# Shares of the edges in free PSUM columns, and the mean for rows without an edge by TensorE instead of GpSimd, in a two-layer sparse graph attention kernel

## What is computed

```python
# layer 0, h = relu(layernorm(x)); input: 6144 x 128, weight: 128 x 128
scores = where(adj > 0, h @ weight @ input.T, NEG_PAD)
x = x + softmax(scores / 0.07, axis=1) @ input
# layer 1, h = relu(layernorm(x)) @ W; valid = adj > 0 and h.sum(1) != 0
e = leaky_relu(h @ a_src [:, None] + h @ a_dst [None, :])
att = where(valid, softmax(where(valid, e, NEG)), 0)
x = x + elu(h + (where(att >= 1e-4, att, 0) * valid.sum(1)) @ h)
```

## Time and profile before

| | |
|---|---|
| median of three runs | 692.81 us (692.28 to 692.93) |
| the profiled execution | 695.36 us, span 693.6 us |
| busy in the span | PE 394.2, DVE 505.4, ACT 407.1, POOL 324.6 us |
| DMA | 186.79 MB, mean 269 GB/s |
| PE clock granted, mean | 0.778 |

### The profile page before, as it was taken

The page is one execution under the profiler, slowest core; times in us unless marked ns, Lnnn a source line. Parts: engine busy times, 40 slices in busy tenths (PEclk is TensorE's granted clock), DMA queues, the critical chain, the costliest instruction groups (busy, mean ns, idle before and its releaser), DMA issues.

```text
span 693.6 us, 9649 instructions
## 1 busy us (share of the span) xinstructions
PE 394.2 (57%) x2916; PEld 267.0 (38%) x2947; DVE 505.4 (73%) x2125; ACT 407.1 (59%) x424; POOL 324.6 (47%) x353
## 2 busy tenths in 40 slices
PE   3244364765867666676758586776370520426654
PEld 1011132342635344443526263545270520426653
DVE  0008868797979898989979898989932642659995
ACT  6348487787798888887988888782220210022232
POOL 6000050523425170706157575757777767778200
PEclk9656596979899999998979889896765565567786
DMA  8999989999899999999899999961221223224322
GB/s 325 410 425 419 385 288 411 343 360 347 299 390 361 387 372 347 393 332 407 305 410 350 393 382 396 379 219 42 63 66 47 60 71 81 49 67 124 101 86 81
DMA packets 37480, 186.79 MB, mean 269 GB/s; under 512 B 7856, under 2 KB 8112, under 8 KB 18864
## 3 DMA queue, kind: packets, MB, share of 16 engines
q1 hardware_dynamic: 28208, 167.02, 62.4%
q0 software_dynamic: 9216, 19.11, 9.9%
HBM read 179.73 MB, written 6.37 MB: 268 GB/s over the span
## 4 chain that ended last, share of the span: by engine, by line
DVE 53%; POOL 12%; issue 11%; PE 11%; DMA 7%; ACT 4%; SPq 0%; DVEq 0%; POOLq 0%
POOL arena L817 7%; DMA arena<-in_adj 6%; PE K L1425 5%; DVE G L1136 3%; DVE keys L1025 3%; DVE RTp L1195 2%; DVE mi_w L1176 2%; ACT R_all L898 2%; DVE cand L1055 2%; POOL X L793 2%; POOL arena L793 2%; DVE cand L1043 1%; DVE stats L1210 1%; ACT arena L869 1%; DVE mi L1178 1%
## 5 line engine op out<-in xcount | busy, mean ns | idle before, releaser
L869 ACT ACTIVATE arena<-arena,half_c 128x2048 fp8e4<-128x2048 int32 x144 | 280.6, 1997 | 29.7 <-DMA arena<-in_adj 22.0
L793 POOL DMA_INDIRECT X<-in_L_gnn_input,idx_all x132 | 129.6, 982 | 270.4 <-DVE idx_near L1107 233.8
L1425 PE MATMUL K<-arena,bits 128*128 128x512 fp8e4 x576 | 168.9, 434 | 52.5 <-ACT arena L869 26.8
L817 POOL DMA_INDIRECT arena<-table,idx_near x96 | 99.7, 1039 | 32.2 <-issue 28.7
L1425 PEld LDWEIGHTS K<-arena,bits 128*128 128x128 bf16 x576 | 59.0, 108 | 94.5 <-ACT arena L869 30.9
L1025 DVE MAX8 keys<-K 128x8 int32<-128x128 f32 x192 | 42.4, 280 | 55.4 <-PE K L1425 55.3
L817 POOL DMA_INDIRECT E<-table,idx_near x48 | 45.5, 947 | 14.6 <-issue 13.7
L1437 PE MATMUL G<-g,R_all 128*128 128x128 bf16 x324 | 25.6, 229 | 32.9 <-DVE G L1136 17.6
L898 ACT CAST R_all<-G 128x512 fp8e4<-128x512 f32 x36 | 19.9, 588 | 38.7 <-PE G L1459 27.3
L1505 PE MATMUL SB<-mi,R_all 128*128 128x6 bf16 x144 | 5.8, 169 | 62.7 <-DVE mi L1178 62.6
L1437 PEld LDWEIGHTS G<-g,R_all 128*128 128x128 fp8e4 x324 | 20.9, 103 | 42.6 <-issue 20.9
(11 more groups left out here) (248 smaller groups left out, 1006.0 us busy)
## 6 DMA issues: line engine op xcount, KB each, us to landing
arena<-in_adj SPq DMA_DIRECT2D x144, 1024.0 KB, 8.4
table<-hs SPq DMA_DIRECT2D x12, 262.0 KB, 8.5
hs<-table SPq DMA_DIRECT2D x12, 262.0 KB, 2.8
E<-in_L_gnn_input SPq DMA_DIRECT2D x1, 3072.0 KB, 25.8
out_x<-x_all SPq DMA_DIRECT2D x12, 256.0 KB, 2.0
x_all<-in_x SPq DMA_DIRECT2D x1, 2560.0 KB, 19.4
X<-in_L_gnn_input,idx_all POOLq DMA_INDIRECT x132, 5.2
arena<-table,idx_near POOLq DMA_INDIRECT x96, 2.6
```

What stands on the lines that cost most here:

```text
L793: pool.indirect_dma_start(out=x_of(b)[:, e, :], out_offset=None, in_=inp, in_offset=bass.IndirectOffsetOnAxis(ap=idx_all[:, at:at + 1], ax ...
L817: pool.indirect_dma_start(out=E[g][:, t, :], out_offset=None, in_=tables[g], in_offset=bass.IndirectOffsetOnAxis(ap=idx_near[:, t, g:g + 1 ...
L869: nc.scalar.activation(sign[:, load % RING, :], ring[:, load % RING, :], ACT.Sign, bias=half_c[:], scale=1.0, saturate=False).then_inc(sig ...
L1425: last = mm(bank_[:], bits[:, third * TB + j, :], sign[:, load % RING, j * FOLD:(j + 1) * FOLD], start=False, stop=(third == G - 1 and j = ...
```

## The change

- POOL's `scale_mean` and `add_mean` go, with their semaphores; `neighbours` issues its twelve gathers in a row.
- DVE makes, at the end of each turn, four matrices `no_row`: the identity scaled by `empty_all` of a tile (`rows_without_edges`). `attend` adds a fourth product for each tile, `no_row` times `mean_b`, into the same accumulation.
- `add_attention` waits for hx_r (ACT has read x) where it waited for mean_added.
- p_e moves from SBUF to columns 288 to 299 of the PSUM bank SB; in layer 1 the last product of `weights2` is written to columns 256 to 279 of S3 (SA or SB), where `shares2` reads it.

```diff
-        mean_w = sb("mean_w", [P, B, D])
+        no_row = sb("no_row", [P, B, P])
-        p_e = sb("p_e", [P, BG])
+        p_e = SB[:, 288:288 + BG]
+
+        def shares_of(i):
+            return S3[i % 2][:, 256:256 + QG]
...
-                def scale_mean(b):
-
-                    if b == 0:
-                        pool.wait_ge(mean_kept, 1)
-                    pool.wait_ge(empty_r, b + 1)
-                    size = SIZES[b]
-                    link(pool.tensor_tensor(mean_w[:, 0:size], mean_b[:].unsqueeze(1).broadcast_to([P, size, D]),
-                                            empty_all[:, tiles(b)].unsqueeze(2).broadcast_to([P, size, D]), ALU.mult))
-
-                def add_mean(b):
-
-                    pool.wait_ge(hx_r, b + 1)
-                    pool.tensor_tensor(x_all[:, tiles(b), :], x_all[:, tiles(b), :], mean_w[:, 0:SIZES[b]], ALU.add
-                                       ).then_inc(mean_added, 1)
-                    pool.wait_ge(mean_added, b + 1)
...
-                    neighbours(n - 1, 0, BG // 2)
-                    if n >= 2:
-                        scale_mean(n - 2)
-                        add_mean(n - 2)
-                    neighbours(n - 1, BG // 2, BG)
+                    neighbours(n - 1, 0, BG)
...
-                scale_mean(NB - 2)
-                add_mean(NB - 2)
                 third_stored(1)
                 records(1, 0, 2 * Q)
-                neighbours(NB - 1, 0, BG // 2)
-                scale_mean(NB - 1)
-                add_mean(NB - 1)
-                neighbours(NB - 1, BG // 2, BG)
+                neighbours(NB - 1, 0, BG)
...
+                def rows_without_edges(b):
+
+                    wait(dve, att_r, b)
+                    for t in range(SIZES[b]):
+                        last = ts(no_row[:, t, :], ident[:], empty_all[:, FROM[b] + t:FROM[b] + t + 1], None, ALU.mult)
+                    last.then_inc(no_row_r, 1)
+
                 def add_attention(b):
 
-                    dve.wait_ge(mean_added, b + 1)
+                    dve.wait_ge(hx_r, b + 1)
...
                     if 0 <= b2 < NB:
+                        rows_without_edges(b2)
                         differences(b2)
...
-                    link(tt(w_e, w_e, spread_shares(i)[:, :, PK - 1], ALU.mult))
+                    link(tt(shares_of(i), w_e, spread_shares(i)[:, :, PK - 1], ALU.mult))
...
-                    w = w_e[:, (j % 2) * BG:(j % 2 + 1) * BG]
+                    w = shares_of(j // 2)[:, (j % 2) * BG:(j % 2 + 1) * BG]
...
                 def attend(b):
 
+                    pe.wait_ge(no_row_r, b + 1)
                     pe.wait_ge(RTp_r, b + 1)
...
                     for t in range(SIZES[b]):
                         for g in range(G):
                             e = t * G + g
-                            last = mm(att_of(b)[:, t * D:(t + 1) * D], RTp[:, e, :], x_of(b)[:, e, :],
-                                      start=(g == 0), stop=(g == G - 1))
+                            mm(att_of(b)[:, t * D:(t + 1) * D], RTp[:, e, :], x_of(b)[:, e, :],
+                               start=(g == 0), stop=False)
+                        last = mm(att_of(b)[:, t * D:(t + 1) * D], no_row[:, t, :], mean_b[:], start=False, stop=True)
                     last.then_inc(att_r, 1)
```

More of the change, by code:

```diff
@@ L593, in fast_path @@
         wt_r, wt_kept, ws_r, mean_r, init_r = sem("wt_r"), sem("wt_kept"), sem("ws_r"), sem("mean_r"), sem("init_r")
-        ws_kept, mean_kept, inp_summed, empty_r, mean_added, RT_r = (sem(s) for s in (
-            "ws_kept", "mean_kept", "inp_summed", "empty_r", "mean_added", "RT_r"))
+        ws_kept, mean_kept, inp_summed, no_row_r, RT_r = (sem(s) for s in (
+            "ws_kept", "mean_kept", "inp_summed", "no_row_r", "RT_r"))
         signed, folded, keys_used = sem("signed"), sem("folded"), sem("keys_used")
@@ L1072, in spread_lists @@
                     tt(over_list[:, 0:size], over_list[:, 0:size], lists[:, 0:size, SLOTS - 1], ALU.max)
-                    ts(empty_all[:, tiles(b)], cum[:, 0, 0:size], 0.0, None, ALU.is_equal).then_inc(empty_r, 1)
+                    ts(empty_all[:, tiles(b)], cum[:, 0, 0:size], 0.0, None, ALU.is_equal)
                     per_third = lists[:, 0:size].unsqueeze(2).broadcast_to([P, size, G, SLOTS])
```

## The result

| | before | after |
|---|---|---|
| median, same chip | 692.54 us (689.64 to 692.93) | 671.62 us (670.22 to 673.45) |
| profiled execution | 695.36, span 693.6 | 671.09, span 669.4 |
| busy DVE, POOL, PE | 505.4, 324.6, 394.2 | 491.8, 285.1, 402.5 |

The account below looks back on a forecast made before the run. The chain of waits was taken as the bound, 53% VectorE and 12% POOL. Terms -20.0 + 5.9 + 1.0 - 8.6 + 1.4 - 1.3 = -21.6 us from 692.8 gave 671.2 us, range 665 to 680.

Parts of the forecast that it names:

- Step 1: Mask part: with the means off POOL, mi_w and mi no longer wait, 2.5 us in each of eight batches, -20.0 us.
- step 2: Mask part: four scaled identities on VectorE cost 0.65 us a batch in nine executions, +5.9 us.
- stall stays: Mask part: twelve gathers in a row hold mi_w and mi as POOL's tensor operations did; 690.2 us, chance 0.03.
- Step 3: Mask part loads: early batches just fit at 35.5 us, the three record batches lose +1.0 us in all.
- DMA takes over: Mask part: loads keep batches from falling below 36.3 us, record batches save nothing; 677.7 us, chance 0.18.
- Step 4: Mask part: four more mean matmuls take 1.0 us on TensorE, hidden under its 1.55 us wait; nothing counted.
- Steps 5 and 6: POOL's chain before the last batch: mean operations gone (7.2 us), gathers no longer held beside products; together -8.6 us.
- step 6: Shares in PSUM let POOL's gathers pass VectorE's products: 1.75 us off POOL's stretch, new scalings +0.3; VectorE's products unchanged.
- The rival that operands don't matter: Gathers beside VectorE's products are not held by their operands, so PSUM columns buy nothing; 674.2 us, chance 0.06.
- The slower kernel: VectorE's product with its share in PSUM runs at half rate, 2.96 us instead of 1.76; 702.7 us, chance 0.02.
- Step 7: Last batch: four more products on the chain cost 1.26 us, scalings 0.1; together +1.4 us.
- Step 8: POOL's records after the last batch: two gathers behind the second layer's products get shorter by 0.55 and 0.73, -1.3 us.

Follow-up runs that it names:

- before_warm: The kernel before the change, with idle matmuls added at the three places where TensorE waits in a batch; 686.12 us, ratio 0.9909.
- warm_records_late: The changed kernel with idle matmuls at TensorE's three waits and the 44 record gathers of the last four mask batches moved behind the mask part; 708.17 us.
- warm_again: The changed kernel with idle matmuls at all three places where TensorE waits, run a second time; 668.27 us against 673.41 for the changed kernel.
- psum_only: The kernel before the change with only the shares moved to PSUM columns, the mean left on POOL; 689.2 us, ratio 0.9952.
- mean_only: The changed kernel with the edges' shares back in SBUF, the mean still on TensorE; 675.59 us, ratio 0.9754.
- no_product: The changed kernel with its scalings but without TensorE's products of mean and scaled identity; 673.46 us, ratio 0.9725.

## Why the prediction was right, and where its steps were not

The total came out within half a microsecond of the forecast, and that is partly luck: in the mask part two terms were wrong, in opposite directions.

- **Step 1** (2.5 us a batch at mi_w and mi) and **step 2** (scalings) hold in sum, with each size a little off. mi_w and mi are at 0.17 in every batch, but the cast between them takes 0.42 instead of 0.17. A tensor_scalar of decode, the 0.44 of the earlier trace rows that step 2 took as its upper price, now takes 0.22. The scalings cost 0.78, not 0.65. The nearest comparison with the clock kept up is before_warm with warm_records_late: the first gather for batch 10 goes from 453.6 to 440.1, -13.5. The steps say -20.0 + 5.9 = -14.1; with the scalings' 0.78 in place of 0.65, -13.0. It is not quite clean, since before_warm still has its record gathers, 0.2 us in each of three batches. The rival "stall stays" (690.2) is out by the rows.
- **Step 3** is the term that was mis-sized: "+1.0 in all for the three of them, out of a possible 3 x 1.9 = 5.7". With the clock up, loads that share the engines with record gathers cost 446.2 to 446.8 against 440.1, so 6.1 to 6.7, more than was called possible. The ring's lead of five loads, which I took for a cushion, did not carry through the last two batches. The rival "DMA takes over" was nearly right for the record batches, where it saw nothing saved: 34.6, 36.3 and 37.3 in warm_again against 36.3 in before_warm. It was wrong for the early ones: it put their floor at 36.3 us, while these ran at 34.5 with 389 to 395 GB/s under idle matmuls, and up to 408 without.
- **A term was missing**, and it has the other sign. The 37.4 us from which steps 1 to 3 count down was not VectorE's own path: 1.27 of it came from the work ahead of the edge lists, the fold above all, at half clock. In the profiled execution that is 10.0 us over the mask part, by the medians 6.8. The changed kernel got rid of it in most batches and kept it in three of 37 us. What it got back is eaten in part by the loads: 447.9 lies 7.8 above the 440.1, and these 7.8 are clock and loads together; no run separates them. So -10.0 - 13.5 + 7.8 = -15.7 in place of -13.1: one error up, one down.
- **Step 4** holds: the fast batches take 34.5 us with the products and without them. TensorE's wait for g, 1.55 in the earlier trace rows, falls to 0.59 to 0.66 in three of the eight batches from 177 to 461 us, as reckoned (0.55), and stays at 1.55 to 1.60 in the others; it vanishes in none.
- **Steps 5 and 6** hold together, -8.6 as said. For step 6, psum_only gives 1.7 in this stretch, as reckoned (1.75). mean_only gives 2.5, since without the mean operations a gather begins sooner under batch 9's RTp (2.29 instead of 1.44). The rival that operands don't matter is out. On this the Trainium skill's inference ("SBUF — State Buffer", section "Who interferes with whom") that a tensor_tensor leaves descriptor generation alone does not hold for these gathers: 2.11 us for a gather under a product with two SBUF operands, 0.94 with one of them in PSUM. The slower kernel (product at 2.96) is out as well: 1.75.
- **Step 7**: VectorE's wait grew by 1.14, where 1.26 was reckoned for the products; the stretch +1.0 for +1.4. How much of the 1.14 is the products and how much the clock is open, as no_product shows. POOL now waits 5.33 for the table store instead of 3.25, since it is done with its own work sooner.
- **Step 8**: -1.0 for -1.3; the two gathers lost 0.55 and 0.73, but the one at 579.79 now takes 1.21, 0.27 over.

What stays open: why the granted clock falls in some batches and not in their neighbours. In both traces of the changed kernel the long batches are ones in which TensorE waits twice ahead of the spread rows, 0.42 to 0.96 us for hs and then 1.55 to 1.60 for g; the batches with one wait of 0.53 to 0.66 for g take 34.5 or 34.6. But the batch from 246.57 has both waits (0.76 and 1.55) and lasts 34.46. That idle matmuls remove the loss is shown; which pause is the decisive one is not.

## What to carry to other kernels

A small VectorE operation of a length that its size can't explain is waiting for someone: look on POOL for an operation that ends when it does, and take that off POOL, for when it was only moved here it found other victims. Where DMA shares stand near 1, a saving per batch is not to be multiplied by the batches: ask from which batch the loads come just in time, and count the saving only up to there. And a wait for TensorE is priced only after a look at the granted clock in that stretch, since a change of schedule alone can give it or take it.

## What the runs showed that was not expected

- POOL's tensor operations also hold a 12-element VectorE product (0.19 to 0.76) and a group of three tensor_scalars (0.40 to 0.90), not the reduction between them (0.35 each time).
- A gather can hold VectorE, not only the other way: the cast between mi_w and mi now ends with the gather that started at 273.89, 0.42 instead of 0.17, in nine of the twelve batches. That takes 0.25 a batch from step 1's gain. Casts begun earlier under a gather ran in 0.17, and so did one that began as late (at 379.38 in warm_again); what decides it is open.
- 36 idle matmuls a batch on TensorE made the kernel 5.1 us faster on the same chip, without taking any work away.
